# Window attention in a four-layer kernel: the two key halves of a score row merged into 32 columns before the softmax, and a new order of the first loads

## The reference, cut to what matters

```
q = (x @ Wq + bq)            # 16 heads of 8
k, v = ...                   # 2 key/value heads of 8, each shared by 8 query heads
pk, pv = pad(k, 16), pad(v, 16)          # 16 zero rows at both ends of the sequence
scores = einsum('bhntd,bhnud->bhntu', qb, kb)      # n: blocks of 32 queries, u: 64 keys
win_mask = (u >= t) & (u < t + 32)
probs = softmax(where(win_mask, scores, -inf))
out = einsum('bhntu,bhnud->bhntd', probs, vb)

x = x + window_attention(layernorm(x))
x = x + ffn(layernorm(x))
x = x + linear_attention(layernorm(x))
x = x + ffn(layernorm(x))
```

## Time and profile before

| | |
|---|---|
| median of 3 runs | 614.67 us (612.76 to 614.82) |
| the profiled execution | 614.55 us, of which the span from first to last instruction is 612.7 us |
| busy share of the span | PE 92%, DVE 83%, POOL 79%, ACT 61% |
| from 140 to 528 us | PE busy 387.27 of 388.00 us |
| one turn in that stretch | 33.05 us |

### The profile page before, as it was taken

One profiled execution on the slowest core, in us unless ns is written; L12 is line 12 of the kernel. 1 busy time (PEld: TensorE's weight loads), 2 busy tenths in 40 slices (PEclk: granted clock), 3 DMA queues, 4 the chain that ended last, 5 costly groups with the idle time before them and its releaser, 6 DMA issues.

```text
span 612.7 us, 16001 instructions
## 1 busy us (share of the span) xinstructions
PE 563.6 (92%) x5972; PEld 356.4 (58%) x5972; DVE 510.3 (83%) x1187; ACT 374.3 (61%) x610; POOL 481.2 (79%) x518
## 2 busy tenths in 40 slices
PE   2478798989999999999999999999999999999976
PEld 1244445555665665666657566566566665777653
DVE  3399997999999999999999999999999999953430
ACT  2144454646767767676766685866767676766532
POOL 1475769679898989989898989898998686867550
PEclk9999997989999999999999999999999999999998
DMA  8410101011111111101101111111110010000001
GB/s 311 114 26 24 40 7 41 7 21 24 22 42 22 40 23 40 24 22 34 28 25 23 36 25 40 22 41 23 40 25 22 18 28 2 13 7 18 1 21 31
DMA packets 29453, 21.08 MB, mean 34 GB/s; under 512 B 8128, under 2 KB 25152, under 8 KB 29376
## 3 DMA queue, kind: packets, MB, share of 16 engines
q1 hardware_dynamic: 28384, 18.57, 11.6%
q10 hardware_dynamic: 992, 1.50, 0.8%
HBM read 9.57 MB, written 4.19 MB: 22 GB/s over the span
## 4 chain that ended last, share of the span: by engine, by line
PE 76%; DVE 13%; POOL 5%; issue 4%; ACT 1%; DVEq 0%; POOLq 0%; ACTq 0%
PE ring L496 17%; PE ring L508 17%; PE ps_o L481 9%; PE ps_s L464 9%; PE ring L445 7%; PE ring L519 4%; PE ring L539 4%; PE ring L576 2%; PE ring L528 2%; DVE masked L992 2%; PE ring L553 2%; DVE shifted_t L1007 2%; PE ring L547 2%; DVE rowmax L1000 2%; POOL xn_P L374 1%
## 5 line engine op out<-in xcount | busy, mean ns | idle before, releaser
L399 POOL TENSOR_TENSOR shifted<-masked,rowmax 128x1024 f32<-128x1024 f32 x64 | 121.8, 1906 | 30.0 <-DVE rowmax L1000 29.5
L992 DVE TENSOR_TENSOR masked<-ps_s,first 128x1024 f32<-128x1024 f32 x64 | 77.2, 1207 | 5.5 <-PE ps_s L464 5.0
L751 ACT ACT_TABLE_LOAD x60 | 77.0, 1283 | 4.7 <-issue 3.6
L1007 DVE STREAM_TRANSPOSE shifted_t<-shifted 128x1024 f32<-128x1024 f32 x64 | 78.7, 1230 | 0.0
L1000 DVE TENSOR_REDUCE rowmax<-masked 128x16 f32<-128x1024 f32 x64 | 76.9, 1202 | 0.7
L464 PE MATMUL ps_s<-kx,q_t 64*32 64x512 f32 x1024 | 70.6, 608 | 3.8 <-DVE masked L992 3.8
L481 PE MATMUL ps_o<-probs_t,vx 32*32 32x256 f32 x2048 | 70.8, 384 | 0.0
L769 ACT ACTIVATE probs_t<-shifted_t 128x1024 f32<-128x1024 f32 x64 | 66.9, 1045 | 3.4 <-DVE shifted_t L1007 2.2
L496 PE MATMUL ring<-xT_G,w1b 128*128 128x512 f32 x128 | 66.8, 611 | 1.1 <-ACT xT_G L741 0.7
L508 PEld LDWEIGHTS ring<-w,hid_F 128*128 128x128 f32 x512 | 58.4, 192 | 12.7 <-issue 12.1
L508 PE MATMUL ring<-w,hid_F 128*128 128x128 f32 x512 | 61.4, 278 | 0.4 <-ACT hid_F L761 0.4
(11 more groups left out here) (107 smaller groups left out, 1058.6 us busy)
## 6 DMA issues: line engine op xcount, KB each, us to landing
kx<-kv_t SPq DMA_DIRECT2D x124, 40.0 KB, 2.1
x_P<-in_x SPq DMA_DIRECT2D x16, 256.0 KB, 2.8
out_x<-x_G SPq DMA_DIRECT2D x16, 256.0 KB, 2.4
vx_t<-kv_t SPq DMA_DIRECT2D x128, 8.0 KB
down_s<-in_down_m SPq DMA_DIRECT2D x6, 256.0 KB, 8.3
up_s<-in_up_m SPq DMA_DIRECT2D x5, 256.0 KB, 8.2
later<-in_later_c SPq DMA_DIRECT2D x1, 648.0 KB, 10.0
up_s<-in_up_m ACTq DMA_DIRECT2D x2, 256.0 KB, 6.7
```

Source lines behind the costliest of these rows:

```text
L399: nc.gpsimd.tensor_tensor(shifted[:, j % 2], masked[:, j % 2], m, ALU.subtract).then_inc(subtracted.sem, 1)
L751: nc.scalar.activation(unused[:, i:i + 1], half[0:1, 0:1], function)
L992: nc.vector.tensor_tensor(masked[:, j % 2].rearrange("p k h u -> p (k h) u"), ps_s[:].rearrange("p k (h u) -> p (k h) u", u=SPAN), band.re ...
L1007: nc.vector.transpose(shifted_t[:, j % 2].rearrange("p k h u t -> p (k h u t)"), shifted[:, j % 2].rearrange("p k h u -> p (k h u)")).then ...
```

## The change

A score row has 32 columns in place of 64 from PSUM on. ACT copies the first half of the keys out of `ps_s` into `merged` (`first_half_out`), DVE copies the last half over it where `last_half` is set (`merge_halves`, a predicated copy), and maximum, subtraction, transpose and exponential all work on 512 elements per partition where they had 1024. The subtraction is now DVE's, in place. POOL then multiplies the 512 probabilities with the two 0/1 masks `keep` into the two halves that PE needs (`probs_parted`, 1024 elements out).

Three other things go with it. `normalise` on POOL makes `nm` and `nmr` for all four streams and all groups, and `xn` is x times `rstd` plus `nmr`; the first `xn_P` is made on DVE. SP loads the second group of x right after `first`, and 7 of its 11 matrices, `vx_t`'s constants and `later` only after it issued the first `kx` transfers. One of the two memsets of `kx` is POOL's. And the order of all engines is written anew, with other PSUM banks.

```
+            def first_half_out(g, j):
+                act.wait_ge(vec.sem, vec.after(g if j >= 2 else g - 1, f"W.tr{(j - 2) % 4}"))
+                act.wait_ge(product.sem, product.after(g, f"W.S{j}"))
+                nc.scalar.activation(merged[:, j % 2].rearrange("p k h t -> p (k h) t"),
+                                     ps_s[:].rearrange("p k (h u) -> p (k h) u", u=SPAN)[:, :, 0:WIN], ACT.Copy
+                                     ).then_inc(halved.sem, 1)
...
-            def add_mask(g, j):
...
+            def merge_halves(g, j):
...
+                dve.wait_ge(halved.sem, halved.after(g, f"W.c{j}"))
+                nc.vector.copy_predicated(
+                    merged[:, j % 2].rearrange("p k h t -> p (k h) t"),
+                    last_half.bitcast(mybir.dt.uint32).rearrange("p (a t) -> p a t", a=1).to_broadcast([P, HEADS, WIN]),
+                    ps_s[:].rearrange("p k (h u) -> p (k h) u", u=SPAN)[:, :, WIN:SPAN]).then_inc(drained["S"].sem, 1)
...
+            def subtract_max(g, j):
+                dve.wait_ge(vec.sem, vec.after(g, f"W.max{j}"))
+                m = rowmax[:, j].rearrange("p (k h a) -> p k h a", k=KV, a=1).to_broadcast([P, KV, HPK, WIN])
+                nc.vector.tensor_tensor(merged[:, j % 2], merged[:, j % 2], m, ALU.subtract).then_inc(vec.sem, 1)
...
-            def subtract_max(g, j):
-                pool.wait_ge(vec.sem, vec.after(g if j >= 2 else g - 1, f"W.tr{(j - 2) % 4}"))
-                pool.wait_ge(vec.sem, vec.after(g, f"W.max{j}"))
-                m = rowmax[:, j].rearrange("p (k h a) -> p k h a", k=KV, a=1).to_broadcast([P, KV, HPK, SPAN])
-                nc.gpsimd.tensor_tensor(shifted[:, j % 2], masked[:, j % 2], m, ALU.subtract).then_inc(subtracted.sem, 1)
+            def probs_parted(g, j):
...
+                pool.wait_ge(product.sem, product.after(g if j >= 2 else g - 1, f"W.PV{(j - 2) % 4}"))
+                pool.wait_ge(probs.sem, probs.after(g, f"W.E{j}"))
+                nc.gpsimd.tensor_tensor(
+                    probs_t[:, j % 2].rearrange("p u k h t -> p u (k h) t"),
+                    probs_m[:, j % 2].rearrange("p (a k) h t -> p a (k h) t", a=1).to_broadcast([P, PARTS, HEADS, WIN]),
+                    keep.rearrange("p (u a t) -> p u a t", u=PARTS, a=1).to_broadcast([P, PARTS, HEADS, WIN]), ALU.mult
+                ).then_inc(parted.sem, 1)
...
                 for j in range(TILES):
-                    last = nc.gpsimd.tensor_scalar(xn[s][:, j], x_of(g, s)[:, j], mv[s][:, j, 0:1],
-                                                   rstd[s][:, j:j + 1], ALU.subtract, ALU.mult)
+                    last = nc.gpsimd.tensor_scalar(xn[s][:, j], x_of(g, s)[:, j], rstd[s][:, j:j + 1],
+                                                   nmr[s][:, j:j + 1], ALU.mult, ALU.add)
```

More of the change, by code:

```diff
@@ L344, in turn @@
                     load_x(g)
+                for g in due(t, 8):
+                    store_y(g)
             for t in range(TURNS):
@@ L743, in _ @@
             place = itertools.count()
+            in_use = [None]
             in_use = [None]
@@ L836, in load_butterflies @@
                 act.dma_start(down_s[INNER - 1][:], down_m[INNER - 1]).then_inc(down_in[INNER - 1], 16)
-            def first_normalised():
-                act.wait_ge(pool_step.sem, pool_step.after(0, "P.nmr"))
-                for j in range(TILES):
-                    last = nc.scalar.activation(xn["P"][:, j], x_of(0, "P")[:, j], ACT.Identity,
-                                                scale=rstd["P"][:, j:j + 1], bias=nmr[:, j:j + 1])
-                last.then_inc(normed.sem, 1)
             def up_stage_out(n, part):
@@ L969, in moments @@
                 last.then_inc(vec.sem, 1)
+                if g == 0 and s == "P":
+                    dve.wait_ge(vec.sem, vec.after(0, "P.mv"))
+                    dve.wait_ge(pool_step.sem, pool_step.after(0, "P.rstd"))
+                    for j in range(TILES):
+                        last = nc.vector.tensor_scalar(xn[s][:, j], x_of(0, s)[:, j], mv[s][:, j, 0:1],
+                                                       rstd[s][:, j:j + 1], ALU.subtract, ALU.mult)
+                    last.then_inc(normed.sem, 1)
             def residual(g, s, name, base):
@@ new lines, in turn @@
+                for g in due(t, 4):
+                    moments(g, "W")
+                if t == 4:
+                    up_outer_stage(1)
+                for g in due(t, 6):
+                    residual(g, "L", "L.proj", "F")
+                for g in due(t, 3):
+                    scores_transposed(g, 2)
+                for g in due(t, 6):
+                    moments(g, "L")
+                for g in due(t, 5):
+                    phi_q_made(g)
+                for g in due(t, 3):
+                    head_outputs(g, 0)
@@ new lines, in turn @@
+                for g in due(t, 3):
+                    head_outputs(g, 1)
+                for g in due(t, 2):
+                    subtract_max(g, 0)
+                for g in due(t, 0):
+                    moments(g, "P")
+                if t == 1:
+                    down_outer_stage(0)
+                for g in due(t, 2):
+                    merge_halves(g, 1)
+                    scores_transposed(g, 0)
+                    row_max(g, 1)
+                for g in due(t, 3):
+                    head_outputs(g, 2)
```

497 lines of the change are left out of this document (248 added, 249 removed), and 54 rows, old and new, of tables (COVERED, PRODUCTS, VECTOR).

## The result

The changed kernel takes 618.37 us (median of 4 runs, 618.17 to 618.70) against 614.66 us before (612.76 to 614.82). The ratio is 1.0068, 95% interval 1.0048 to 1.0088: slower by 0.7%, where 599 us had been forecast. The profiled execution has a span of 616.3 us (before 612.7) and a granted clock of 0.972 (0.986).

What follows compares the result with a forecast made beforehand. PE was taken to bound the steady turns (33.05 us) and DVE the fill. Start -3.5, fill -9.7 and drain -2.2 sum to -15.4 against 614.55, so 599 us (by the terms' bounds 590 to 607); range 586 to 632.

Steps and rivals of the forecast that it cites:

- Steady turn, 33.05 us, PE without a gap: Steady stretch: PE's turn stays 33.05 us and PE busy throughout, with DVE at 27.9 and POOL at 31.1 us.
- `xn` at 0.46 us: POOL's norms: multiply and add near 0.46 us for 128 columns, where the old pair took 0.78, 16 times a turn.
- POOL's sum: POOL per steady turn: 31.0 + 1.8 + 2.4 + 1.2 - 5.3 = 31.1 us, under PE's 33.05.
- Multiplication 2.36 us: POOL's mask multiplication of 1024 columns: 2.36 us, between ends of 1.90 and 2.36; +1.8 us a turn.
- Predicated copy 0.60: DVE's copy of the last half, 512 columns: 0.60 us, upper end 1.13 if it makes two passes.
- Drain -2.2: Pipeline's end: three norms on the chain, each 0.7 us shorter, gain 2.2 us; with `xn` as before, +1.8.
- Fill -9.7: From 43.50 to 140 us: 14 tiles, each 0.69 us shorter on DVE, gain 9.7 us; bounds -14.3 and 0.
- DVE sets the pace for 14 tiles: In the fill, 43.50 to 140 us, DVE bounds all 14 tiles, so its 0.69 us saved per tile counts.
- Start -3.5: Before the first product with the values: an earlier second x gains 3.5 of 9.5 us; bounds 0 and -9.5.
- No earlier than before: At the start: `later` lands behind the keys, so the third x, issued at 27.63 us, comes no earlier.
- DVE becomes the bound by waiting behind POOL: Rival, steady turns: DVE's two-input operations wait behind POOL's, turn 34.7 us at 1.0 us each, 630 us; chance 0.12.
- The fill does not move: Rival, fill: longer path to scores' release, `later` and third x no sooner; 612 us (608 to 616); chance 0.12.

Runs made afterwards that it cites:

- e2: The changed kernel with the old normalisation on POOL (subtract, then multiply; without `nm` and `nmr`): 628.28 us, ratio 1.0218 to the kernel before.
- e4: The kernel before with only the new normalisation on POOL (multiply and add, two small steps more): 615.61 us, ratio 1.0017.
- e12: The changed kernel with POOL's mask multiplication made a one-input multiplication by 1.0 over the same 1024 outputs, leaving out the masking: 603.82 us, ratio 0.9827 to the kernel before.
- e1: The changed kernel with DVE's subtraction of the row maximum replaced by a second, one-input maximum of the same 512 elements: 610.51 us, ratio 0.9931 to the kernel before.
- e11: The changed kernel with a tiny reduction in place of DVE's subtraction of the maximum: 605.57 us, ratio 0.9850 to the kernel before.
- e3: The changed kernel with `later` loaded ahead of the first keys instead of behind the matrices: 613.04 us, ratio 0.9956 to the kernel before.
- e7: The kernel before with only the second x issued right behind `first`: 607.19 us, ratio 0.9898; run again, 608.62 us, ratio 0.9903.
- e6: The changed kernel with `later` ahead of the first keys and the third x right behind them: 611.25 us, ratio 0.9971 to the kernel before.
- e13: The changed kernel with all matrices and `later` issued ahead of the first keys, as in the kernel before: 612.36 us, ratio 0.9963 to the kernel before.
- e16: The changed kernel with a second maximum in place of DVE's subtraction, and `later` and the third x early: 605.44 us, ratio 0.9852 to the kernel before.
- e18: The changed kernel with one maximum a row, `later` and third x early, and DVE's subtraction also accumulating an unused sum: 605.61 us, ratio 0.9834 to the kernel before.
- e14: The changed kernel with one maximum for all 16 heads of a row, so a one-tensor-input subtraction: 613.47 us, ratio 0.9981 to the kernel before.
- e15: The changed kernel with one maximum a row, a one-tensor-input subtraction, and `later` and third x early: 608.94 us, ratio 0.9903 to the kernel before.

## Why the prediction was wrong, step by step

- *Steady turn, 33.05 us, PE without a gap*: right, but for the gap of 1.56 us at 485. DVE 30.02 us in it (27.9 foreseen), POOL 29.89 (about 31).
- *`xn` at 0.46 us*: right, the commonest lengths are 452 and 453 ns; those over 600, which make the mean of 530 in the group shown, lie beside a subtraction of DVE. No row of the kernel before shows the -5.3 us that stand for it in POOL's sum; the runs do, 0.45 us against the 0.78 of the old form. Why the pair of operations matters no run shows. e2 shows that this term carries the change: with the old form the turn is 34.0 us. I had put that case between 33.4 and 37.6.
- *Multiplication 2.36 us*: right, 2387 ns. *Predicated copy 0.60*: right, 0.61 from start to start (the merge at 318.00 us), a record of 0.72.
- *Drain -2.2*: right, -2.1, and the same part alone gives it in e4.
- *Fill -9.7*: wrong, +2.2 up to the 17th batch of PV and +4.4 up to the last. The step that failed is "0.32 us of waiting each. I add this to the subtraction: 2.72 us per tile". That mean was that of `o_w`, a short operation in another order of POOL. Measured from start to start: 0.61 + 0.60 + 1.19 + 0.62 = 3.02 us, and `o_w` waits 0.25 longer than before: 3.3 us a tile against 3.41. The relief was to be 0.69 us a tile, and about one subtraction in four pays 2.2 us for it, as POOL's multiplications fall where DVE subtracts. By the mean alone the fill would still gain 14 x 0.14 = 2 us. That it lost goes with where the waits fall: PE stands 5.3 us for `ps_s` in two places (before 1.0). How much of the loss is those waits was not parted from the rest.
- *DVE sets the pace for 14 tiles*: not borne out. In e12, where the waits are small, fill and turns take 9.4 us less than before, nearly the forecast, though up to 4.7 of that can be the clock's. But the same sum gives e1 a gain of 14 x 0.62 = 8.7 us, and it had 3.2; e11 about 15, and it had 7.3. That e12 agrees may be luck.
- *Start -3.5*: wrong, +1.3, and e3 prices the error at 5 us. Two steps failed. "No earlier than before" was taken for no later: `later` went from the end of one queue to behind the keys and the matrices, and landed at 27.6 us; in e7, where it kept its place, POOL went on at 19.68. And the 12.4 us from the third x's issue to the first PV, for which I had no row, are 15.8, as before (15.9) and in e7 (16.1). About 2.7 of the 15.8 are the lower clock: 0.87 + 0.97 + 0.87 us in the three batches from 33.81 us on. Sent out earlier still, in e3 and e6, the third x waits longer for the rest.
- *The rivals*: "DVE becomes the bound by waiting behind POOL" had the right mechanism in the wrong place. I priced it only from where the steady turn breaks, 33.05 us, and it never got there. The case in between, waits too small for the turn and large enough for the fill, was named as a bound ("0, if longer waits ... eat it") and given no chance of its own. "The fill does not move" comes nearest; its `later` and third x did come no sooner, but its 612 us has no start and no fill that lose.
- *Two sums*: the terms' own bounds add up to 589 and 612, not to 590 and 607. And eight waits of 1.2 us make a turn of 36.3, so about 648 us by the same sum that gave 630, not 635.

The account of the 19 us between 599 and 618.4: 5 at the start (e3, e13), 8 in the subtraction (e1; 5 to 7 by e16 against e6), and the rest, 6 us, perhaps in the waits of `o_w` and its like, since e12, which shortens both, gives 14.6. That last part was not tried by itself.

Why e18 works where e14 gives half is a rule of the Trainium skill ("SBUF — State Buffer", Who interferes with whom): on VectorE two-tensor operations and the fast two-port form of `tensor_scalar` use ports that GpSimd shares, `tensor_reduce` and the form with an accumulator don't. The traces agree: 2.84 and 2.58 us for the first two behind a multiplication, 0.67 and 0.73 for the others. By the same section any GpSimd instruction that reads SBUF shuts out a VectorE one with two SBUF inputs until it ends. In e12 it did not: beside a 2.8 us multiplication with one tensor input such subtractions took 1.52 us when they began 0.1 us behind its start and 0.68 from 1.1 us on, and the measurement decides.

## What to carry to other kernels

When work moves between VectorE and GpSimd, price each VectorE operation at its own length plus the GpSimd operation it can fall behind, at the places where the two orders meet, and look for a form that does not wait, even one that is slower alone. A constant that is loaded later must be followed to every engine that waits for it and to the transfers those engines release. And a moved line (here the second x, 1%) can be worth more than the rewrite it came with: undo the parts one by one.

## What the hardware showed that I had not expected

- A `tensor_scalar` of 128x512 on VectorE with one tensor input takes 0.48 us alone and 2.58 behind GpSimd's two-input multiplication; with an accumulator output it takes 0.73 + 0.08 and never waits. The slower form made the kernel 0.7% faster (e18 against e15, each against the kernel before).
- On GpSimd a multiplication of 128x1024 by a constant takes 2.80 us, longer than with two tensors (2.39), yet VectorE's two-input subtractions that began 1.1 us or more behind its start did not wait (0.68 us, 11 of 11).
- The clock puts some us between two profiles in a place where nobody changed anything: after waits of 2.56 and 2.77 us the same two batches of eight matmuls took 4.92 and 5.40 us at a granted clock of 0.75 and 0.68 in the kernel after, and 3.70 each at 1.00 in e6. What decides it the runs do not show.
- On GpSimd `tensor_scalar` with multiply and add takes 0.46 us for 128 columns where subtract and multiply took 0.78.
- A predicated copy of 128x512 out of PSUM costs 0.61 us from start to start, the same as a plain operation.
